# A new order for the instructions of five engines, in a fused attention and feed-forward kernel

## What is computed

```python
x = L0_attn_t                                   # (16, 1024, 256)
x = x + _layernorm(_L0_attn_ref(_layernorm(x), W_qkv, b_qkv))
x = x + _layernorm(_L0_ffn_ref(_layernorm(x), w_gate, w_up, w_down))

# attention: qkv = t @ W_qkv.T + b_qkv; softmax(Q @ K.T / 16) @ V
# feed-forward, with integer weights times 1/127:
gate = jnp.einsum('bsd,hd->bsh', x, wg)
up = jnp.einsum('bsd,hd->bsh', x, wu)
h = jax.nn.silu(gate) * up
return jnp.einsum('bsh,dh->bsd', h, wd)
```

## Time and profile before

| | |
|---|---|
| median of 3 runs | 1322.65 us (1322.42 to 1323.86) |
| the profiled execution | 1322.73 us |
| its span, first to last instruction | 1320.9 us |
| granted TensorE clock | 1.00 throughout |
| busy: TensorE / its weight loads | 1308.1 (99%) / 705.6 (53%) |
| busy: VectorE / ScalarE / POOL | 953.1 (72%) / 1019.5 (77%) / 997.6 (76%) |
| chain that ended last, by engine | PE 90%, POOL 3%, ACT 2%, DMA 2%, SP's queue 1%, VectorE 1% |
| transfers issue to landing, median: `yTl` / `PTl` / load of x / `store` | 3.2 / 3.3 / 4.6 / 2.9 us |

### The profile page before, as it was taken

The page is one execution under the profiler, slowest core; times in us unless marked ns, Lnnn a source line. Parts: engine busy times, 40 slices in busy tenths (PEclk is TensorE's granted clock), DMA queues, the critical chain, the costliest instruction groups (busy, mean ns, idle before and its releaser), DMA issues.

```text
span 1320.9 us, 23123 instructions
## 1 busy us (share of the span) xinstructions
PE 1308.1 (99%) x7204; PEld 705.6 (53%) x7204; DVE 953.1 (72%) x2670; ACT 1019.5 (77%) x1610; POOL 997.6 (76%) x1081
## 2 busy tenths in 40 slices
PE   8999999999999999999999999999999999999998
PEld 5455455555555555455554555545555555555655
DVE  7877686776867768687686867767687686766566
ACT  6768787788878788787887877878777887867655
POOL 4887687786868868687786877878778686875645
PEclk9999999999999999999999999999999999999999
DMA  6887657676656865578666776666767666666422
GB/s 203 158 172 143 147 93 145 130 153 116 120 124 134 167 119 112 122 138 161 125 115 124 130 148 128 142 124 111 144 128 158 116 119 121 136 132 130 92 64 65
DMA packets 492110, 171.96 MB, mean 130 GB/s; under 512 B 473041, under 2 KB 475473, under 8 KB 491986
## 3 DMA queue, kind: packets, MB, share of 16 engines
q1 hardware_dynamic: 491184, 169.67, 65.1%
q10 hardware_dynamic: 802, 0.79, 0.2%
HBM read 36.70 MB, written 16.78 MB: 40 GB/s over the span
## 4 chain that ended last, share of the span: by engine, by line
PE 90%; POOL 3%; issue 2%; ACT 2%; DMA 2%; SPq 1%; DVE 1%; POOLq 0%; ACTq 0%; DVEq 0%
PE S L1073 71%; PE S L1232 17%; POOL Pl L449 1%; DMA yTl<-yl 1%; SPq L309 1%; DMA PTh<-Ph 1%; POOL qTl L426 0%; POOL yl L476 0%; PE S L1102 0%; PE S L1155 0%; ACT xh L558 0%; SPq L278 0%; ACT P L614 0%; SPq L321 0%; POOL xl L401 0%
## 5 line engine op out<-in xcount | busy, mean ns | idle before, releaser
L449 POOL TENSOR_TENSOR Pl<-P,Ph 128x1024 f16<-128x1024 f32 x128 | 271.4, 2131 | 52.4 <-issue 37.8
L1073 PE MATMUL S<-PTh,xh 128*128 128x512 f16 x512 | 194.1, 379 | 0.0
L1073 PE MATMUL S<-PTl,xh 128*128 128x512 f16 x512 | 194.0, 379 | 0.0
L1073 PE MATMUL S<-PTh,xl 128*128 128x512 f16 x512 | 194.0, 379 | 0.0
L651 ACT ACTIVATE hf<-S,sc 128x512 f32<-128x512 f32 x192 | 129.3, 684 | 64.8 <-PE S L1073 52.8
L614 ACT ACTIVATE P<-P,nmx,sc 128x1024 f32<-128x1024 f32 x112 | 138.2, 1234 | 43.4 <-DVE nmx L901 43.2
L1073 PE MATMUL S<-Wh,hTh 128*128 128x256 f16 x768 | 170.2, 273 | 0.4 <-DVE X L986 0.4
L1073 PE MATMUL S<-Wh,hTl 128*128 128x256 f16 x768 | 170.2, 273 | 0.0
L364 POOL TENSOR_TENSOR rs<-rs,mhalf 128x4 f32<-128x4 f32 (+2 forms) x160 | 146.0, 912 | 13.3
L485 POOL TENSOR_TENSOR hTl<-hf,hTh 128x512 f16<-128x512 f32 x128 | 146.8, 1157 | 8.6 <-ACT hTh L658 5.6
L895 DVE CUSTOM_DVE_ANT_0 P<-S,P 128x512 f32<-128x512 f32 x112 | 76.9, 689 | 96.7 <-ACT P L581 46.6
(11 more groups left out here) (206 smaller groups left out, 3295.6 us busy)
## 6 DMA issues: line engine op xcount, KB each, us to landing
xs<-in_L_attn_t SPq DMA_DIRECT2D x32, 512.0 KB, 4.6
X<-in_L_attn_t SPq DMA_DIRECT2D x32, 512.0 KB, 4.6
out_x<-X SPq DMA_DIRECT2D x62, 256.0 KB, 2.9
PTh<-Ph SPq DMA_TRANSPOSE x128, 3.7
PTl<-Pl SPq DMA_TRANSPOSE x128, 3.3
hTh<-in_L_ffn_w_up SPq DMA_DIRECT2D x1, 768.0 KB, 6.9
hTl<-in_L_ffn_w_down SPq DMA_DIRECT2D x1, 768.0 KB, 8.4
hTl<-in_L_ffn_w_gate SPq DMA_DIRECT2D x1, 768.0 KB, 9.8
```

The costliest lines, as they stand in the source:

```text
L449: p.engine.tensor_tensor(out=Pl[:, m % 3, :], in0=P[:, m % 4, :], in1=Ph[:, m % 3, :], op=ALU.subtract).then_inc(pl_vector if i in PL_ON_V ...
L1073: done = t.engine.matmul(out, s, m, start=(start and i == 0), stop=(stop and i == len(terms) - 1))
```

## The change

The five lists are written in another order: the loop, the start and the last three blocks. No call is added or removed, no argument of a call changes, and no helper, buffer, bank or waited-for value. The prologue of TensorE is unchanged. Of some 1,400 lines of the diff, these are the ones that the prediction speaks of.

SP, the start and the loop:

```diff
             load_x(s, 0, 0)
             load_x(s, 0, 1)
+            load_ffn(s, 2)
             load_x(s, 1, 0)
-            load_ffn(s, 1)
-            load_ffn(s, 2)
             load_x(s, 1, 1)
             load_ffn(s, 0)
+            load_ffn(s, 1)
+            load_x(s, 2, 0)
             turn_x(s, 1, 0, 0)
-            load_x(s, 2, 0)
...
             for b in range(1, 13):
+                turn_x(s, b + 2, 0, 0)
                 turn_p(s, b + 1, 1, 0)
-                turn_x(s, b + 2, 0, 0)
                 turn_x(s, b + 2, 0, 1)
-                turn_p(s, b + 1, 2, 0)
                 turn_y(s, b, 0, 0)
                 turn_y(s, b, 0, 1)
+                turn_p(s, b + 1, 3, 0)
+                turn_p(s, b + 1, 2, 1)
                 turn_x(s, b + 2, 1, 0)
                 turn_x(s, b + 2, 1, 1)
-                turn_p(s, b + 1, 2, 1)
+                turn_p(s, b + 1, 3, 1)
                 turn_t(s, b + 2, 0, 0)
+                turn_p(s, b + 1, 2, 0)
...
             turn_y(s, 15, 1, 1)
+            store(s, 15, 0, 0)
+            store(s, 15, 0, 1)
             store(s, 14, 1, 0)
             store(s, 14, 1, 1)
-            store(s, 15, 0, 0)
-            store(s, 15, 0, 1)
             store_last(s, 0)
```

ScalarE, the start, the loop (three places) and the end:

```diff
             o_high(a, 0, 0, 1)
-            z_high(a, 1, 1, 0)
             p_high(a, 0, 7)
             p_high(a, 1, 0)
+            z_high(a, 1, 1, 0)
...
                 o_high(a, b + 1, 1, 1)
                 copy_u3(a, b + 2, 2)
-                exp(a, b + 2, 3)
-                p_high(a, b + 2, 3)
-                o_high(a, b + 1, 1, 0)
                 y_hat(a, b + 1, 0, 0)
                 y_hat(a, b + 1, 0, 1)
                 y_high(a, b + 1, 0)
+                o_high(a, b + 1, 1, 0)
...
                 p_high(a, b + 2, 5)
+                h_high(a, b + 1, 1, 2, 0)
+                h_high(a, b + 1, 1, 3)
+                silu(a, b + 1, 1, 4, 6)
+                silu(a, b + 1, 1, 5, 2)
                 p_high(a, b + 2, 6)
-                silu(a, b + 1, 1, 4, 6)
-                h_high(a, b + 1, 1, 2, 0)
-                silu(a, b + 1, 1, 5, 2)
-                h_high(a, b + 1, 1, 3)
```

POOL keeps `y_low` behind two `p_low` in the loop. VectorE, the loop:

```diff
                 sum_21(v, b + 2, 3)
+                row_inverse(v, b + 2, 0)
                 sum_22(v, b + 2, 3)
                 x1_add(v, b + 1, 1, 0)
```

TensorE, the loop:

```diff
                 attend_part(t, b + 1, 0, 4, (hmul_done, 12 * b + 11))
+                attend_part(t, b + 1, 0, 5)
                 pair_first(t, b + 2, 0, ...)
-                attend_part(t, b + 1, 0, 5)
                 pair_second(t, b + 2, 0)
                 attend_part(t, b + 1, 0, 6)
                 pair_third(t, b + 2, 0)
                 attend_part(t, b + 1, 0, 7)
                 attend_part(t, b + 1, 0, 0, (silu_done, 12 * b + 11))
-                attend_part(t, b + 1, 0, 1)
                 pair_last(t, b + 2, 0)
                 pair_first(t, b + 2, 1, ...)
                 pair_second(t, b + 2, 1)
+                attend_part(t, b + 1, 0, 1)
+                pair_third(t, b + 2, 1)
                 attend_part(t, b + 1, 0, 2)
-                pair_third(t, b + 2, 1)
+                attend_part(t, b + 1, 0, 3)
                 attend_part(t, b + 1, 1, 4, (ol_done[1], 2 * b + 3))
-                attend_part(t, b + 1, 0, 3)
-                attend_part(t, b + 1, 1, 6)
                 pair_last(t, b + 2, 1)
                 project_v(t, b + 1, 0, (ft_done[0], 4 * b + 2), (ft_done[1], 4 * b + 2))
+                attend_part(t, b + 1, 1, 6)
                 pair_first(t, b + 2, 2, ...)
+                attend_part(t, b + 1, 1, 0, (ol_done[0], 2 * b + 3))
                 pair_second(t, b + 2, 2)
-                attend_part(t, b + 1, 1, 0, (ol_done[0], 2 * b + 3))
```

More of the change, by code:

```diff
@@ L1418, in _ @@
-            turn_p(s, 1, 5, 1)
-            turn_p(s, 1, 4, 0)
+            turn_p(s, 1, 1, 1)
+            turn_t(s, 2, 1, 0)
+            turn_p(s, 1, 4, 0)
+            load_x(s, 3, 1)
+            turn_p(s, 1, 4, 1)
+            turn_p(s, 1, 5, 0)
+            turn_t(s, 2, 1, 1)
+            turn_p(s, 1, 5, 1)
+            turn_p(s, 1, 6, 0)
             turn_p(s, 1, 7, 0)
+            turn_p(s, 1, 7, 1)
             turn_p(s, 1, 6, 1)
-            turn_p(s, 1, 7, 1)
+            turn_p(s, 2, 0, 1)
@@ L1454, in _ @@
-                reload(s, b + 1, 0)
-                turn_p(s, b + 1, 6, 1)
-                turn_p(s, b + 1, 5, 1)
-                turn_p(s, b + 1, 7, 1)
-                load_x(s, b + 3, 1)
-                turn_p(s, b + 1, 7, 0)
+                reload(s, b + 1, 0)
+                load_x(s, b + 3, 1)
+                turn_p(s, b + 1, 5, 1)
+                turn_p(s, b + 1, 6, 1)
+                turn_p(s, b + 1, 7, 1)
+                turn_p(s, b + 1, 7, 0)
+                turn_p(s, b + 1, 6, 0)
@@ L1470, in _ @@
             turn_y(s, 13, 0, 1)
+            turn_p(s, 14, 2, 0)
             turn_x(s, 15, 1, 0)
@@ L1840, in _ @@
             y_hat(a, 1, 0, 1)
+            o_high(a, 1, 1, 1)
             o_high(a, 1, 1, 0)
@@ L2044, in _ @@
             silu(a, 15, 0, 2, 2)
+            h_high(a, 15, 0, 0)
             y_hat(a, 15, 1, 0)
@@ L2123, in _ @@
             z_float(v, 1, 1, 0)
+            row_inverse(v, 0, 0)
             ffn_low(v, 1)
@@ L2150, in _ @@
             h_mul(v, 0, 0, 0, 0)
+            row_inverse(v, 1, 0)
             z_rest(v, 2, 0, 6)
@@ L2325, in _ @@
             sum_11(v, 15, 2)
-            o_low(v, 14, 1, 0)
+            row_inverse(v, 14, 1)
             sum_22(v, 15, 2)
             sum_12(v, 15, 2)
-            row_inverse(v, 14, 1)
+            o_low(v, 14, 1, 0)
             o_low(v, 14, 1, 1)
@@ L2337, in _ @@
             x1_add(v, 14, 1, 0)
+            row_inverse(v, 15, 0)
             sum_22(v, 15, 3)
@@ L2612, in second_part @@
             gate_up(t, 15, 0, 2, 2, (silu_done, 180), (hl_vector, 60), three)
-            down(t, 14, 1, 1, (x1_done, 128), three)
             down(t, 14, 1, 0, (x1_done, 126), three)
@@ L2616, in second_part @@
             gate_up(t, 15, 0, 4, 0, (silu_done, 182), (hmul_done, 182), three)
+            down(t, 14, 1, 1, (x1_done, 128), three)
             gate_up(t, 15, 0, 5, 2, (silu_done, 183), (hl_vector, 61), three)
```

552 lines of the change are left out of this document (269 added, 283 removed).

## The result

The changed kernel took 1327.82 us (median of 7 runs, 1326.75 to 1328.64) where the kernel before took 1322.45 (7 runs, 1321.95 to 1323.86). The ratio is 1.0039, with a 95% interval of 1.003 to 1.0049: slower, by more than a measurement of this kernel leaves open. The forecast was no change, 1322.3, with a range up to 1324.9; the time lies above that range.

A forecast was written before the change was run, and what follows sets the result against it. TensorE was taken to bound the kernel, busy for all 80.51 us of a good pass. Late y −1.24, tight places +0.26, weights 0, `attend(0,1,0)` +0.4 and last block +0.15 gave −0.43, so 1322.3 us; range 1320.8 to 1324.9.

The forecast's parts named there:

- The late y: Loop: y turned earlier, so `gate_up(b,0,0)` no longer waits for its low half in three passes; −1.24 us.
- Tight places: Loop: four TensorE waits come close to zero slack, costing 0.02 us a pass, +0.26 in all.
- lose in every pass: Rival: `pair_second` waits for a later `copy_m1` and `pair_last` inherits it, 0.3 us a pass, +3.9, 1325.9; chance 0.18.
- head (a): Start: `load_ffn(2)`, 768 KB, moved behind the first two x loads, beside the weights' transfer; 0 taken, bounds 0 to +1.3.
- weights late: Rival: nine tenths of ffn's load go ahead of the weights on the shared engines, +1.1 us, 1323.4; chance 0.11.
- Head (b): Start, around 62 us: two `p_high` ahead of `z_high(1,1,0)` delay a low p transfer for `attend(0,1,0)`; +0.4 us, bounds 0 to +0.8.
- Head (c): Start: the other short waits stay, as TensorE itself releases their producers in the same order; nothing, ±0.1 us.
- The last block: End: `add_bias(15,0,1)` ahead of the two last `h_high` makes `h_rest` late for a matmul; +0.15 us, bounds 0 to +0.4.

The follow-up runs named there:

- new loop and mended joint: Kernel before with the new loop, `turn_p(14,6,0)` behind `turn_p(14,4,0)` and block 15's last `z_part` ahead of `gate_up(13,0,5)`: 1321.86 us.
- the mended start: Changed kernel with five start steps moved, the `w_down` load back among them: 1323.51 us; a second kernel also had `z_high(3,1,2)` three places further ahead: 1326.36.
- the move of y with its third piece: Kernel before with `project_v`, `y_hat` and `y_high` earlier in the loop, plus `attend_part(b+1,0,3)` ahead of `attend_part(b+1,1,4)`: 1340.69 us.

## Why the prediction was wrong

**The late y: right in place, and gone for good.** The step said `yl` issued over 5 us before its use. In the pass shown it was issued at 736.02 for a use at 741.87, 5.85 ahead, and landed 3.7 later:

```profile
736.02 1.24 SPq L315 DMA_TRANSPOSE yTl<-yl  x1
```

```profile
741.87 0.38 PE L1073 MATMUL S<-yTh,Gh 128*128 128x512 f16 x1
```

With the 0.24 of slack in the earlier trace rows that 3.7 would have been late. The eight traces with the new loop have 104 places `gate_up(b,0,0)` for b = 1 to 13 and no late y at any; the six traces with the old one have 3 to 6 late ones each, 0.69 to 1.92 us in sum. So "all late ones go" holds. "All three have one cause" holds only for the last link. In before, y's own transfer was slow just at 1140.54 (4.0 us to landing); at 495.49 and 657.10 it took its usual 3.2 and 3.3, but was issued 0.7 and 0.9 us later in its pass than in the good ones. ScalarE's `p_high` ahead of y had waited 1.8 us for another transfer, of p, instead of 0.44, and with it `y_high` and `y_low` came late:

```profile
485.40 1.06 ACT L621 ACTIVATE Ph<-P 128x1024 f16<-128x1024 f32 x1 [1.80 <-DMA PTh<-Ph]
```

```profile
490.06 2.13 POOL L476 TENSOR_TENSOR yl<-yn,yh 128x1024 f16<-128x1024 f32 x1 [1.34 <-ACT yh L641]
```

The slack that the move gave covers both. That the gain is −1.24 in a typical run is not shown: runs of before scatter, and the one with new loop and mended joint came out 0.5 us under its before. What the step left out is that its own sentence ("so it gains no wait") depends on the rest of the loop's order; taken alone the same moves cost 20 us.

**Tight places: right, and the rival "lose in every pass" is out.** `copy_m1` ended 0.08 before `pair_second` (said 0.06), the sum 0.07 before its `pair_last` (said 0.07), and no pass but the first takes more than 80.54. In after, ScalarE's and TensorE's rows (700.36 + 0.57 = 700.93, against 701.01), and VectorE's last step before `pair_last` (it ends at 706.12, against 706.19):

```profile
700.36 0.57 ACT L581 ACTIVATE P<-S 128x512 f32<-128x512 f32 x1
```

```profile
701.01 0.38 PE L1232 MATMUL S<-tTh,qTh 128*128 128x512 f16 x1
...
706.19 0.39 PE L1232 MATMUL S<-xTh,qTh 128*128 128x512 f16 x1
```

```profile
705.37 0.75 DVE L895 CUSTOM_DVE_ANT_0 P<-S,P,mxh 128x512 f32<-128x512 f32 x1
```

A value that is there 0.07 us ahead costs nothing behind another score product. +0.26 was said, +0.1 came.

**The failed step is head (a).** It said: "Bounds 0 to +1.3; I take 0, since the part of the weights that has landed by then is not held up at all." It was +1.56 for the transfer, over the upper bound, and +1.56 for the clock, which had no price at all. Three things failed in it. The share was worked out in even bytes, "at most half of that, 1.05", when with rows of 3 KB beside rows of 1 KB `w_down` got nearly two thirds of them, and the weights landed 2.5 us later, against a slack of 1.0; the rival "weights late" had this, with +1.1. Why they came even later than if all of `w_down` had gone ahead of them (10.34, for 10.1 in the step) is not known. The idle engine: the step wrote the 0.82 between the end of the transfers and 8.82 off as slack, and never asked what TensorE does in a longer gap. In after the fill matmuls end at 7.92 (in before at 9.03), so the gap was 2.46. And the clock behind the gap doubled the bill. With both, the rival would have said 1322.3 + 3.1 = 1325.4, just beyond the range.

**Head (b): right place, too small.** `attend(0,1,0)` waits for the low p transfer, 0.61 for a forecast of 0.4 and bounds of 0.8. Moving its cause back removes it (0.61 gone in the mended start), making it alone in the kernel before brings it (0.85), though a smaller one also stands in the two kernels with more fill work, where that step isn't moved (0.26, 0.44).

**Head (c): wrong.** "The other short waits of the head stay ... Nothing, ±0.1" stood for 0.84 + 0.34 + 0.46 + 0.10, less the 0.49 that went: +1.25. The 0.84 is a late landing that is there in after and in one kernel with the mended start, but not in the kernel with the load alone put back nor in the other mended one; what brings it is open. The 0.34 and the 0.46 stay with the load put back and are gone with the old start, so they are of the new order. I walked one pass of the loop step by step and no stretch of the start, where many lines move by more places than in the loop. The same holds for the end, "the waits of TensorE beside the last pair of score tiles stay": `h_rest(14,1,5,2)` behind two `x1_add` is one line of the diff, and costs 0.76 there; with it put back the wait is gone, but 0.61 of it came back at the next one.

**The last block: right size, wrong cause.** +0.15 was said for `add_bias`, +0.22 came, and stayed with `add_bias` back behind the last `h_high`. By the trace it is the move of `h_low(15,1,0)` on POOL, which the step didn't look at; no run moved that line alone.

**The sum, then:** −1.24 + 0.1 + 3.12 + 0.61 + 1.25 + 0.76 + 0.22 + 0.12 (the two `project_v`) = 4.94, against −0.43.

## What to carry to other kernels

- In a reordered kernel the loop is the part that was looked at most; walk the start, the end and the joints line by line too, since a queue's order holds across them (3.05 us for one transfer that stood ahead of the one ScalarE needed, 0.76 for one `h_rest`).
- A load moved ahead on one queue takes more of the wires the longer its rows are. Compare row lengths, not bytes alone: 768 KB in 3 KB rows took 1.8 times the bytes of its neighbour over 3 us and made it land 2.5 us later; the same 768 KB in 1 KB rows made it land 0.9 later, within its slack. And price new idle time of TensorE in the start twice, once for the wait and once for the clock after it: here 1.56 and 1.56 on the path to the first z product.
- Moves that make a value earlier have no price of their own: the same lines cost 20 us in one order and stand in another that costs nothing.

## What the hardware showed that was not expected

- After 2.46 us without a matmul in the start the granted clock stood at 0.50 for some 3 us; a product of 1.95 took 3.51. After 2.15 us without one, in the kernel before with the early load, it fell 1.2 us into the product. With the gap cut to 1.31 by fill work the clock stayed at 1.00 and the product took 1.99. These are one trace each.
- That is not the whole rule: in the profiled runs of both kernels with the mended start the clock fell to 0.50 at about 13 us too, behind waits of some 0.43 and 0.52. In every trace it also stands at 0.50 at the very end, behind TensorE's last matmul, where it costs nothing. It fell early even in a kernel whose start is that of before, line for line (the move of y with its third piece, 0.50 from 12.6 to 16 us). In the kernel with only the load moved back, and in two with the old start and the new loop, it stayed at 1.00 behind the same two waits. So the order of the start doesn't decide it; what does is open.
- The 24 fill matmuls took 5.30 us in before and 4.22 in after, with nothing changed in them, and between 4.1 and 5.3 in the others. In before they start 0.213 us apart all the time, in after only until 6.7 us and then 0.109, half of that, both under a granted clock of 1.00. No run here explains it.
- The transposing transfer of y's low part landed 3.0 us after its issue in before and 4.7 in after at the same step (0.84 us of TensorE's time). Over all traces it took 3.0 to 4.8, with a median of 3.2. Late y were more frequent in the kernels whose start was shifted by 1.7 to 2.7 us (five and six places, 1.92 us) than in before (three, 1.24), but the kernel with `w_gate` early, with no shift, has five as well (1.37): one trace each does not tell a pattern.
